# The last stage of a mixture-of-experts layer: TensorE sums every second tile instead of every third

## The reference

```python
logits = x @ router_weight.T
probs = softmax(logits)
top_v, top_i = top_k(probs, 8)
for w_gu, w_d, c in experts:              # c: weight of this expert for each token, 0 if not chosen
    gate, up = split(x @ w_gu.T)
    y = silu(gate) * up @ w_d.T
    acc = acc + c[:, None] * y
x = x + tanh(g_ffn) * acc                 # x before the second layernorm
```

## Time and profile before

| | before |
|---|---|
| median of 3 runs | 753.8 us (747.69 to 755.25) |
| profiled execution, its own time | 744.94 us |
| its span | 743.0 us |
| last stage, from the first load of `ACC` | 689.58 to 743.0 us |
| busy in the whole span | PE 545.1, DVE 496.3, ACT 436.4, POOL 366.3 us |

### The profile page before, as it was taken

One profiled execution on the slowest core, in us unless ns is written; L12 is line 12 of the kernel. 1 busy time (PEld: TensorE's weight loads), 2 busy tenths in 40 slices (PEclk: granted clock), 3 DMA queues, 4 the chain that ended last, 5 costly groups with the idle time before them and its releaser, 6 DMA issues.

```text
span 743.0 us, 14469 instructions
## 1 busy us (share of the span) xinstructions
PE 545.1 (73%) x4084; PEld 436.2 (59%) x4084; DVE 496.3 (67%) x1345; ACT 436.4 (59%) x911; POOL 366.3 (49%) x441
## 2 busy tenths in 40 slices
PE   0399798898898988673238788788878787984255
PEld 0266565666565655452038777687778777974244
DVE  2567778788878887632567666666666676673477
ACT  4467766677767777552207666666666676686300
POOL 8411165556655554445713555555555546656000
PEclk9999989989989999777559999999999999998587
DMA  6887787678766679211356776777677777751896
GB/s 144 187 211 205 194 242 205 191 191 211 216 186 183 174 168 290 68 64 64 113 152 184 233 221 199 223 215 212 205 228 220 211 211 222 216 152 70 344 411 270
DMA packets 66465, 146.88 MB, mean 198 GB/s; under 512 B 13065, under 2 KB 33567, under 8 KB 64368
## 3 DMA queue, kind: packets, MB, share of 16 engines
q1 hardware_dynamic: 47600, 97.71, 46.9%
q0 software_dynamic: 16208, 45.42, 18.4%
q10 hardware_dynamic: 2608, 3.15, 1.9%
HBM read 90.34 MB, written 60.06 MB: 202 GB/s over the span
## 4 chain that ended last, share of the span: by engine, by line
PE 37%; DVE 21%; ACT 14%; another core or an unknown queue 9%; issue 9%; DMA 6%; POOL 2%; SPq 1%; ACTq 1%; DVEq 0%; POOLq 0%
PE ST L1434 8%; DVE MX L798 7%; PE SC L1643 6%; PE OX L1451 6%; PE SC L1414 6%; ACT PE_T L1338 4%; PE ST L1655 4%; DVE OT L1127 3%; DMA out_dram<-OT 3%; ACT PE_T L1223 2%; ACT XTP L1304 2%; PE OX L1655 2%; DVE XTP L1033 2%; PE ST L1629 2%
## 5 line engine op out<-in xcount | busy, mean ns | idle before, releaser
L740 POOL DMA_INDIRECT y_rows<-PE_T,IDXE x128 | 135.2, 1056 | 137.6 <-ACT XTP L1304 67.6
L798 DVE TENSOR_REDUCE MX<-SC 128x4 f32<-128x1024 f32 x128 | 154.4, 1215 | 48.4 <-PE SC L1414 43.9
L1223 ACT ACTIVATE PE_T<-ST 128x512 f32<-128x512 f32 x256 | 139.2, 598 | 77.7 <-PE ST L1434 69.2
L686 POOL DMA_INDIRECT x_rows<-XN,IDX x128 | 125.6, 981 | 95.8 <-PE ST L1434 38.7
L1643 PE MATMUL SC<-XTP,WP 128*128 128x320 f32 x768 | 131.6, 323 | 0.2 <-issue 0.2
L1434 PE MATMUL ST<-QC,KP 128*128 128x256 f32 x512 | 114.2, 343 | 12.5 <-ACT PE_T L1223 9.1
L1643 PEld LDWEIGHTS SC<-XTP,WP 128*128 128x128 f32 x768 | 122.2, 202 | 0.7 <-issue 0.4
L1434 PEld LDWEIGHTS ST<-QC,KP 128*128 128x128 f32 x512 | 81.2, 213 | 50.8 <-ACT PE_T L1223 23.7
L1414 PE MATMUL SC<-KP,QC 32*128 32x256 f32 x512 | 63.0, 348 | 53.5 <-DVE MX L798 27.3
L1054 DVE TENSOR_TENSOR PE_T<-SC,PE_T 128x320 f32<-128x320 f32 x64 | 31.4, 491 | 82.0 <-ACT PE_T L1318 61.1
L1414 PEld LDWEIGHTS SC<-KP,QC 32*128 32x128 f32 x512 | 41.5, 209 | 70.2 <-DVE MX L798 34.7
(11 more groups left out here) (160 smaller groups left out, 809.0 us busy)
## 6 DMA issues: line engine op xcount, KB each, us to landing
W<-experts_dram SPq DMA_DIRECT2D x64, 384.0 KB
XE<-x_rows SPq DMA_DIRECT2D x64, 288.0 KB
ACC<-y_rows SPq DMA_DIRECT2D x16, 1024.0 KB, 9.8
x_rows<-FILL POOLq DMA_DIRECT2D x16, 576.0 KB
QC<-q_scr SPq DMA_DIRECT2D x56, 128.0 KB
X<-x_rows SPq DMA_DIRECT2D x64, 72.0 KB
k_scr<-KS SPq DMA_DIRECT2D x16, 256.0 KB
q_scr<-QS SPq DMA_DIRECT2D x16, 256.0 KB
```

The costliest lines, as they stand in the source:

```text
L686: pool.indirect_dma_start(x_rows, bass.IndirectOffsetOnAxis(ap=IDX[:, rows, k:k + 1], axis=0), XN2[:, rows, :], None).then_inc(dispatched[ ...
L740: pool.indirect_dma_start(y_rows, bass.IndirectOffsetOnAxis(ap=IDXE[:, n % YS, j:j + 1], axis=0), Y[:, n % YS, j, :], None, bounds_check=T ...
L798: nc.vector.tensor_reduce(MX[:, u // 4].rearrange("p r (j g) -> p j r g", j=2)[:, :, :, group(u) % 4], SC[:, u % 2, :, :].rearrange("p j ( ...
L1223: nc.scalar.activation(PE_T[:, h % EXP_RING, :], ST[:, j, :], ACT.Exp, scale=SCALE).then_inc(exp_done, 1)
```

## The change

`folds(t)` becomes t % 2 == 1: PE sums tiles 1, 3, ..., 15, eight instead of five, in four PSUM banks in turn instead of two. DVE sums tiles 0, 2, ..., 14 in four pairs, (0, 2), (4, 6), (8, 10) and (12, 14); the lone tile is gone. `DIAG` has 64 matrices instead of 40. `add_fold` of the folded tiles 2m - 2 and 2m - 1 (that is, tiles 4m - 3 and 4m - 1) stands behind `pair(m)`, and the last two behind those of the last pair. `OT` has four places for folded tiles. A store of a pair now writes two tiles that don't lie beside each other. The ring `ACC` keeps its six places.

```diff
--- before.py
+++ after.py
@@ -41,7 +41,7 @@
 SLOTS = 8
 WS = 4
 PRODUCTS = ((0, 0), (0, 1), (1, 0))
-FS = 7
+FS = 8
 YS = 4
 
 NO = max(k * (min(TOK, TOK * K8 // k) - MAIN + P - 1) // P + E - k for k in range(1, E + 1) if TOK * K8 // k > MAIN)
@@ -109,7 +109,7 @@
 
 def folds(t):
 
-    return t % 3 == 2
+    return t % 2 == 1
 
 
 def build(nc, x, keys, vals, g_attn, g_ffn, rwt, wexp, out, debug=None):
@@ -229,7 +229,7 @@
         DIAG = sb("DIAG", [P, len(FOLDS) * K8, P])
 
         def fold_ps(t):
-            return SC[:, t // 3 % 2, 0, 0:D]
+            return SC[:, t // 2 % 2, t // 4 % 2, 0:D]
 
 
         SC = ctx.enter_context(nc.psum_tensor("SC", [P, 2, 2, 512], F32))
@@ -349,8 +349,7 @@
         summed = sem("summed")
         added = sem("added")
         pair_out = [sem(f"pair_out{n}") for n in range(2)]
-        fold_out = [sem(f"fold_out{n}") for n in range(2)]
-        last_out = sem("last_out")
+        fold_out = [sem(f"fold_out{n}") for n in range(4)]
 
         SP_H, DVE_H, POOL_H, ACT_H = held
 
@@ -591,17 +590,16 @@
             for t in range(TILES):
                 of = t - AR
                 if of >= 0 and folds(of):
-                    sp.wait_ge(folded, of // 3 + 1)
+                    sp.wait_ge(folded, of // 2 + 1)
                 elif of >= 0:
-                    sp.wait_ge(summed, 2 * K8 * (of // 3 + 1))
+                    sp.wait_ge(summed, 2 * K8 * (of // 4 + 1))
                 sp.dma_start(ACC[:, t % AR].rearrange("p k d -> p (k d)"),
                              y_rows[t * P * K8:(t + 1) * P * K8, :].rearrange("(p k) d -> p (k d)", k=K8)
                              ).then_inc(acc_in[t % AR], 16)
-            pairs = TILES // 3
             for h in range(2):
-                sp.wait_ge(pair_out[h], 16 * len(range(h, pairs, 2)))
-                sp.wait_ge(fold_out[h], 16 * len(range(h, pairs, 2)))
-            sp.wait_ge(last_out, 16)
+                sp.wait_ge(pair_out[h], 16 * len(range(h, TILES // 4, 2)))
+            for h in range(4):
+                sp.wait_ge(fold_out[h], 16 * len(range(h, len(FOLDS), 4)))
 
 
         @block.gpsimd
@@ -1133,23 +1131,21 @@
                 need(dve, pair_out[m % 2], m // 2 * 16)
                 for k in range(K8):
                     for a in range(2):
-                        weigh_row(3 * m + a, k, 2 * (m % 2) + a, 2 * K8 * m + 2 * (k - 1) + a + 1)
+                        weigh_row(4 * m + 2 * a, k, 2 * (m % 2) + a, 2 * K8 * m + 2 * (k - 1) + a + 1)
 
             def add_fold(m):
 
-                need(dve, fold_out[m % 2], m // 2 * 16)
+                need(dve, fold_out[m % 4], m // 4 * 16)
                 need(dve, folded, m + 1)
-                nc.vector.tensor_tensor(OT[:, 4 + m % 2, :], fold_ps(3 * m + 2), X[:, 3 * m + 2, :], ALU.add).then_inc(added, 1)
-
-            pairs = TILES // 3
-            for m in range(pairs):
+                nc.vector.tensor_tensor(OT[:, 4 + m % 4, :], fold_ps(2 * m + 1), X[:, 2 * m + 1, :], ALU.add).then_inc(added, 1)
+
+            for m in range(TILES // 4):
                 pair(m)
                 if m:
-                    add_fold(m - 1)
-            for k in range(K8):
-                weigh_row(TILES - 1, k, 6, 2 * K8 * pairs + k)
-                if k == K8 // 2:
-                    add_fold(pairs - 1)
+                    add_fold(2 * m - 2)
+                    add_fold(2 * m - 1)
+            for m in range(2):
+                add_fold(TILES // 2 - 2 + m)
 
 
         @block.scalar
@@ -1378,23 +1374,26 @@
             act.wait_ge(gated, 1)
             for t in FOLDS:
                 for k in range(K8):
-                    nc.scalar.activation(DIAG[:, t // 3 * K8 + k, :], IDENT[:, :], ACT.Identity,
+                    nc.scalar.activation(DIAG[:, t // 2 * K8 + k, :], IDENT[:, :], ACT.Identity,
                                          scale=W8[:, t * K8 + k:t * K8 + k + 1]).then_inc(diag, 1)
 
-            def store(at, n, to, done):
-                act.dma_start(out[at * P:(at + n) * P, :].rearrange("(a p) d -> p a d", p=P), OT[:, to:to + n, :]).then_inc(done, 16)
-
-            pairs = TILES // 3
-            for m in range(pairs):
+            def fold_store(m):
+                t, to = 2 * m + 1, 4 + m % 4
+                act.wait_ge(added, m + 1)
+                act.dma_start(out[t * P:(t + 1) * P, :], OT[:, to, :]).then_inc(fold_out[m % 4], 16)
+
+            def pair_store(m):
                 act.wait_ge(summed, 2 * K8 * (m + 1))
-                store(3 * m, 2, 2 * (m % 2), pair_out[m % 2])
+                act.dma_start(out.rearrange("(t p) d -> p t d", p=P)[:, 4 * m:4 * m + 3:2, :],
+                              OT[:, 2 * (m % 2):2 * (m % 2) + 2, :]).then_inc(pair_out[m % 2], 16)
+
+            for m in range(TILES // 4):
+                pair_store(m)
                 if m:
-                    act.wait_ge(added, m)
-                    store(3 * m - 1, 1, 4 + (m - 1) % 2, fold_out[(m - 1) % 2])
-            act.wait_ge(added, pairs)
-            store(3 * pairs - 1, 1, 4 + (pairs - 1) % 2, fold_out[(pairs - 1) % 2])
-            act.wait_ge(summed, 2 * K8 * pairs + K8)
-            store(TILES - 1, 1, 6, last_out)
+                    fold_store(2 * m - 2)
+                    fold_store(2 * m - 1)
+            for m in range(2):
+                fold_store(TILES // 2 - 2 + m)
 
 
         @block.tensor
@@ -1692,10 +1691,10 @@
 
             def fold(t):
 
-                m = t // 3
+                m = t // 2
                 need(pe, diag, m * K8 + K8)
                 need(pe, acc_in[t % AR], (t // AR + 1) * 16)
-                need(pe, added, m - 1)
+                need(pe, added, m - 3)
                 for k in range(K8):
                     mm = nc.tensor.matmul(fold_ps(t), DIAG[:, m * K8 + k, :], ACC[:, t % AR, k, :],
                                           start=(k == 0), stop=(k == K8 - 1))
```

## The result

The changed kernel took 749.85 us (median of 20 runs), the kernel before 746.7 in 20 runs beside it: a ratio of 1.005, 95% interval 1.0026 to 1.0075. It is slower by 3.7 us, between 1.9 and 5.6. The forecast was 0.8 us slower and "the same"; its mechanism is there, its size was too small. Its time, 755 us, was counted from the median of three runs, 753.8 us; 20 runs put the kernel before at 746.7, so that 749.85 lies in the range of 748 to 761 says little about the working. The profiled executions took 747.19 and 744.94 us, 2.25 us apart.

A forecast was written before the change was run, and what follows sets the result against it. Loads were taken to pace the last stage; tile 14 landing at 734.1 and the tail put the end at 743.8, 0.8 us over 743.0. Added to the 753.8 us median, that gave 755 us, range 748 to 761.

The forecast's parts named there:

- DVE's 9.6 us: Last stage: DVE loses 24 weighing operations at 0.40 us each, none on the path before the tail.
- PE's more work: Last stage: three more tiles at 3.69 to 5.93 us each, 11 to 18 us, covered by the stream of loads.
- the loop of pair and load: Last stage: each round is a DVE pair, then the load waiting for it, 11.5 us against the DMA engines' 11.4.
- 5.05 + 0.34: Loads waiting for a pair: 5.05 us to land on an empty queue, plus 0.34 us for stores beside them.
- the two pauses: Load queue: empty about 1.1 us each round, stores filling it; short DMA dips near 707, 719 and 730.
- PE's last fold at 3.69 us: Tail: PE sums tile 15 from 737.0 with its clock up, taking 3.69 us, until 740.7.
- ACT's 64 matrices: Start of the last stage: 64 instead of 40 at 0.29 us, ending at 701.1 instead of 694.0, costing nothing.
- The ring: Last stage's load buffers: three loads in flight, 7.5 us, cover a pair's 6.06 us; each round takes 11.5 us.
- The tail: From tile 14's landing to the end: 9.7 instead of 10.2 us, 2.2 of it behind the last add.
- the DMA engines as the only pace: Rival, last stage: loads never pause, stores set the rest; likely 2 us under the kernel before; 17%.
- The last fold at the low clock: Rival, tail: PE's fold of tile 15 takes 5.93 us, end at 745.5, 2.5 over the kernel before; 14%.
- The short ring's far end: Rival, loads 6, 10, 14: 7.0 us each, end 5 to 7.3 over; 21%, of which 5% beyond 1%.

The follow-up runs named there:

- second profile: The changed kernel run again with no edit: last stage 55.3 us, whole-time ratio to the kernel before 1.0003 (0.9977 to 1.0028).
- pooled ratio: Three ratios of the unedited changed kernel to the kernel before, weighed by their intervals: 1.0028, give or take 0.0016.
- third profile: The changed kernel run a third time with no edit: last stage 55.4 us, whole-time ratio to the kernel before 1.003 (0.9996 to 1.0064).

## Why the prediction was right in its mechanism and too small

Its steps, each counted from the first load's issue (689.58 and 690.02):

| step | forecast | measured |
|---|---|---|
| tile 6 lands | 21.5 | 21.3 |
| tile 10 lands | 33.0 | 32.7 |
| tile 14 lands | 44.5 | 45.0 |
| tile 15 lands | 47.4 | 48.4 |
| PE's last fold ends | 51.1 | 52.1 |
| DVE's last add ends | 52.0 | 52.6 |
| end of the span | 54.2 | 55.3 |

The landing of tile 15 is where PE started on it, 738.44, which agrees with its load's issue and time (729.1 + 9.3).

*Right:* that DVE's 9.6 us and PE's more work lie off the path; the loop of pair and load, with its price (5.05 + 0.34 against 5.4 and 5.3) and its round (11.5 against 11.44 and 11.37); the two pauses, their places, and the stores in them; PE's last fold at 3.69 us; that ACT's 64 matrices cost nothing, though they ended at 703.6 and not at 701.1, 2.3 us ahead of the first store. A ring of seven took the loss away, a ring of four put the same round into the kernel before.

*Where it failed, first:* the step "The ring", in its term for the stores beside a load, 0.34 us, which the third round used once more. It was an average of the kernel before, where stores come spread out. Now three at a time pile up. While load 14 was under way they took 0.8 us of the engines, and it landed 6.2 us after its issue instead of 5.4. Tile 10 had landed 0.3 to 0.4 us earlier than in the sum, so tile 14 came 0.5 later. Taking away half of the folded tiles' stores gave the 0.8 us back.

*Where it failed, second:* the step "The tail", which put the end 2.2 us behind the last add and left a term at nothing: "The stores of tiles 9 and 11, held back to the tail, cost nothing more". For the DMA engines that is so, but ACT issues the last five stores one behind the other, half a microsecond apart. The first and the last of the five issues and DVE's adds, in the first profile of the changed kernel and in the second:

```profile
741.04 0.39 ACTq L1387 DMA_DIRECT2D out_dram<-OT  x1
...
742.99 0.47 ACTq L1383 DMA_DIRECT2D out_dram<-OT  x1
```

```profile
630.23 1.41 DVE L1140 TENSOR_TENSOR OT<-SC,X 128x256 f32<-128x256 f32 x4
630.34 0.39 ACTq L1387 DMA_DIRECT2D out_dram<-OT  x1
...
632.29 0.46 ACTq L1383 DMA_DIRECT2D out_dram<-OT  x1
```

The last add ends at 742.66 in the first and at 631.64 in the second, 0.33 and 0.65 us ahead of the last issue, yet that issue comes 1.95 us behind the first in both. So the pair (12, 14) and ACT's five issues set the end, not tile 15, PE's last fold or its add, on which the forecast's path ran. From the landing of tile 14 to the end it is 10.3 us in all three profiles of the changed kernel, with the ring of seven and without the four stores; the forecast had 9.7. That tile 15 landed 1.0 us later than forecast cost nothing here.

The two terms, 0.5 us of tile 14's landing and 0.6 of the tail, are the 1.1 us by which the stage is longer than the sum (55.3 against 54.2). Against the kernel before, tile 14 landed 1.7 us later (45.0 against 43.2) and the tail was 0.1 longer, where the forecast had 1.3 later and 0.5 shorter. The stages differ by 1.1 to 1.9 us, the pooled ratio says some 2, and the first result says 3.7; what of the 3.7 lies beyond the stage is not located. A forecast of 0.8 us within 1% was thus of the right sign; a loss of half a percent that 20 runs tell from nothing was more than it allowed for. The statement that such a measurement can tell 1% was itself too coarse: with 20 runs a quarter of a percent could be told.

*The rivals:* the DMA engines as the only pace (2 us faster) fell with the two holes. The last fold at the low clock did not come: it took 3.69 us in all three profiles of the changed kernel, behind pauses of 1.7 to 1.9 us. Its condition, a pause of more than 2.5 us, would not have been enough either: folds behind 2.9 us (third profile, 720.21) and 3.05 us (second, 621.60) also took 3.69. The Trainium skill's tale of bursts that each start at the low clock ("TensorE: Matmul & The Clock Gate", oscillation) holds here for the folds that start at 714.40 and 726.70, behind pauses of 3.3 and 3.5 us, at a granted clock of 0.50 to 0.56 (as in the stretches from 718 and 730 above), and not for the last one. The short ring's far end, 7.0 us a load, was not seen, but load 14's 6.2 lies halfway to it. The Trainium skill's fixed cost of about 2.0 us plus the bytes ("DMA: Bandwidth & Descriptors", anatomy of one DMA), 4.4 us by estimate, was again less than the 5.0 of load 0 and the 5.3 of a load beside a store.

## What to carry to other kernels

Moving work to an idle engine changes which transfers wait for whom. Count, for every group of work that frees buffers together, how many loads remain in flight while it runs: their transfer time must cover the group's time and the part of a load's time that is not transfer (here 6.1 + 2.5 us against three loads of 2.5), or rounds pay for the rest. In this stage, by one profile, freeing the buffers one by one was worth more than the faster order of operations (0.40 against 0.52 us each). Stores that are issued in clusters delay the loads behind them more than their average says, and at the end the issuing engine's own time counts: five stores at half a microsecond each took longer than the last sum.

## What the runs showed of the hardware

The runs were made on more than one chip, and the same program took different times there. The changed kernel's span was 634.6 us on chip 0 and 733.2 on chip 7; in the first profile it was 745.3. The last stage agreed within 0.1 us. Of the 111 us between the first two profiles, 33 lie before the first matmul of the experts' weights (L1642, at 381.8 against 349.2) and 78 in the expert stage. What the activation of each expert waits for there (`gate`, L1314), first in the first profile (480 to 660 us), then in the second (420 to 560), for whom, us in total, times, longest:

```profile
ACT PE_T L1314 <- remote: 49.7, 16, 4.8
```

```profile
ACT PE_T L1314 <- PE SC L1642: 3.5, 17, 0.2
```

PE is busy 140.00 of 140 us at full clock in the second profile and 149.31 of 180, at a granted clock of 0.92, in the first. The DMA engines moved 288 against 212 GB/s. What releases ACT's activation there, "remote", the profile doesn't name, and why the chips differ no run here settles.
